# Register loads of table places, four at a time among a super's matmuls, and the residual input read behind the last super

## The chip, the cores and the metric

One core of a Trainium2 chip runs the whole kernel. The metric is the device time of one execution in microseconds (us). The kernel before was timed three times: 801.56, 800.24 and 801.06 us, median 801.06 us. The engines are TensorE (PE; PEld is its loading of weights), VectorE (DVE), ScalarE (ACT), GpSimd (POOL) and SyncE (SP, which here only issues DMAs). Each engine has a sequencer that reads its program, works on registers, waits for semaphores and hands work to the engine; a "q" behind an engine's name in a row (PEldq, SPq, DVEq) means a record of the sequencer.

## The reference

One layer of a graph network with a residual sum and a layer norm, on 6250 nodes of 256 features and 100,000 edges of 64 features:

```
sums   = segment_sum(edge_attr, src)                # 6250 x 64
counts = segment_sum(1, src)
agg    = sums / max(counts, 1)
h      = relu([x, agg, u[0]] @ W1 + b1)             # 448 -> 512
y      = h @ W2 + b2                                # 512 -> 256
out    = layernorm(x + y)
```

Everything is float32. The edge features are split into three bfloat16 parts that add up to the float32 value, so that matmuls with bfloat16 one-hot matrices sum them exactly.

## The kernel before

The nodes are held as 125 partitions by 50 columns; two columns together are a bucket (25 buckets). The kernel has four stages.

1. A short setup (to about 28 us) counts the edges of each bucket and works out where each group of up to four edges of a bucket goes.
2. The edge stage (to about 447 us) reads the edges in 44 chunks of 6 batches. For each batch PE sorts the rows with one-hot matmuls (line 858), ACT copies them out of PSUM and POOL scatters them with an indirect DMA to `sorted_rows` in DRAM, in order of bucket. Beside it PE multiplies the node features with the first 256 rows of W1 into `pre`.
3. The super stage (452.5 to 671.5 us) is the one that the change touches. A super is 128 sorted rows with four slots of one edge each, all of one bucket. There are 258 of them, in 129 pairs. SP reads a pair in one DMA of 396 KB (`super_turn` of SP, line 505, the issue at line 511). DVE writes one-hot matrices of 128 by 256 (line 1236; three for the first super of a pair and four for the second; ACT makes the one left, lines 713 and 716). PE adds the super's rows into the table in PSUM: per super 4 slots (`r`) x 2 halves of the nodes (`h`) x 3 parts = 24 matmuls (line 936), each with its own load of weights.
4. The last stage (to 799.5 us), 25 steps `g` of two columns: means, the edge part of the first layer, ReLU, second layer (line 990), residual sum and layer norm, and the stores.

**The order within the super stage.** PE, DVE and ACT each run 16 turns of a hardware loop, one turn being 16 supers (`BODY`), and two supers behind the loop. Where a super's sums go is a column of PSUM that is known only at run time. It is looked up in `where_row`, one partition of SBUF with 384 places for PE and as many row numbers for SP. At the head of each turn PE loads 16 places at once into 16 registers (`pe.load`, line 927). Then for each super: line 929 copies the place of this super from its register, line 930 waits for DVE's one-hots (`s_hot_d`), line 932 for ACT's in every first super of a pair, and the matmuls follow; the column of the second half (`h` = 1) is the place plus 512, computed between the third and the fourth matmul (recorded at line 936). The last matmul raises `s_added`. Four one-hot buffers (`HOT_BUFS`) stand between DVE and PE: DVE and ACT may write the one-hots of super n once super n - 4 is added (lines 1234 and 712). SP may read a pair into its buffer once the pair eight before it is added (line 510), and has its own loads of 8 row numbers per turn (`find_rows`, line 503).

**The residual input.** SP reads `x` again into `xs` (6.4 MB, in the layout of the output) during the super stage: from turn 3 on, behind the eight pairs of each turn, a piece of four columns in two DMAs (112 and 13 partitions, lines 524 to 528), and the last two columns at lines 530 to 532. All of them raise `s_xs`. POOL waits for all 13 pieces (line 614) and then adds `b2` to `xs`, column by column in place: `add_b2` (line 616, its additions at line 619) three steps ahead of the steps of the last stage. Between them POOL makes the low part of the hidden values for the second layer (`low_hidden`, line 628). DVE needs `xs` of a step at line 1296.

Of the kernel before, what the change touches and what calls it, by code (L numbers as in the profile page):

```python
# [9 lines left out]
I32 = mybir.dt.int32  # L10
# [7 lines left out]
P = 128  # L18
NODES, DIM = 6250, 256
# [5 lines left out]
NP = 125  # L25
COLS = NODES // NP
BUCKETS = COLS // 2
ROW = FEAT + 1
XPART = 112
# [35 lines left out]
SUPER_PAIRS = -(-SUPERS // 2)  # L65
# [8 lines left out]
SUPER_COLS = -(-SUPERS // P)  # L74
# [19 lines left out]
PAIR_BUFS = 8  # L94
HOT_BUFS = 4
BODY = 2 * PAIR_BUFS
SUP_TURNS = SUPER_PAIRS // PAIR_BUFS
ACT_SLOT = SLOTS - 1
TURN = 3
TURNS = CHUNKS // TURN  # L100
# [5 lines left out]
LOOKS = -(-(BATCHES - SOON) // LOOK)  # L106
assert LOOKS + 3 <= CHUNKS

X_TURN = 3
X_COLS = 4  # L110
X_PIECES = COLS // X_COLS
X_PIECE = X_COLS * DIM
B2_AHEAD = 3
Z_BUFS = 3
assert X_TURN + X_PIECES + 1 == SUP_TURNS

STEPS = COLS // 2
PAIR = 10
# [4 lines left out]
def build(nc, x, src, attr, u, w1, b1, w2, b2, out):  # L123
# [7 lines left out]
    x_v = x.rearrange("(p c) d -> p (c d)", p=NP)  # L131
# [4 lines left out]
    with ctx:  # L136
        def sb(name, shape, dt=F32):
            return ctx.enter_context(nc.sbuf_tensor(name, shape, dt))
# [7 lines left out]
        def sem(name):  # L146
            return ctx.enter_context(nc.semaphore(name))

        ident = sb("ident", [P, P])
        b2_all = sb("b2_all", [P, DIM])  # L150
        eps_col = sb("eps_col", [P, 1])
        where_row = sb("where_row", [1, 2 * SUPER_COLS * P], I32)
        node_of = sb("node_of", [P, 2 * P], I16)
        pre = sb("pre", [P, COLS * HID // P * NP])
        stats = sb("stats", [P, 2, 2, 6])
# [119 lines left out]
        xs = sb("xs", [P, COLS * DIM])  # L275
# [88 lines left out]
        s_apart = sem("s_apart")  # L364
        s_added = sem("s_added")
        s_table = sem("s_table")
        s_xs = sem("s_xs")
        s_xb = sem("s_xb")
        s_own_act = sem("s_own_act")
        s_own_dve = sem("s_own_dve")  # L370
# [33 lines left out]
        def _(sp):  # L404
# [100 lines left out]
            def super_turn(m, count=PAIR_BUFS, found=False):  # L505
                if not found:
                    find_rows(m, count)
                for k in range(count):
                    at = sp.snap(row_regs[k], min_val=0, max_val=ZERO_SUPER * P)
                    sp.wait_ge(s_added, m * BODY + (2 * k + 2))  # L510
                    sp.dma_start(sup_pair[k][:, :, :, :].rearrange("p s r w -> p s (r w)"),
                                 sorted_rows[bass.ds(at, 2 * P), :].rearrange("(s p) w -> p s w", p=P)
                                 ).then_inc(s_sup[k], 16)
# [4 lines left out]
                sp.wait_ge(s_sent[s], 16 * CHUNKS)  # L518

            super_turn(0, found=True)  # L520
            for m in range(1, X_TURN):
                super_turn(m)
            sp.wait_ge(s_pre, COLS + 1)
            with sp.Fori(X_TURN, X_TURN + X_PIECES) as m:
                super_turn(m)
                for lo, hi in ((0, XPART), (XPART, NP)):
                    sp.dma_start(xs[lo:hi, bass.ds(m * X_PIECE - X_TURN * X_PIECE, X_PIECE)],
                                 x_v[lo:hi, bass.ds(m * X_PIECE - X_TURN * X_PIECE, X_PIECE)]).then_inc(s_xs, 16)
            super_turn(X_TURN + X_PIECES)
            for lo, hi in ((0, XPART), (XPART, NP)):  # L530
                sp.dma_start(xs[lo:hi, X_PIECES * X_PIECE:COLS * DIM], x_v[lo:hi, X_PIECES * X_PIECE:COLS * DIM]
                             ).then_inc(s_xs, 16)
            super_turn(SUP_TURNS, SUPER_PAIRS - SUP_TURNS * PAIR_BUFS)

            def store_step(g, b):
                sp.wait_ge(s_out, g * 2 + 2)
# [10 lines left out]
        def _(pool):  # L547
# [63 lines left out]
                pool.wait_ge(s_w_hi, 3)  # L611
                nc.gpsimd.tensor_tensor(low, whole, high.bitcast(F32), ALU.subtract).then_inc(s_w_lo, 1)
            pool.wait_ge(s_b2, 16)
            pool.wait_ge(s_xs, 2 * 16 * (X_PIECES + 1))

            def add_b2(g):
                for c in range(2 * g, 2 * g + 2):
                    column_x = xs[0:NP, c * DIM:(c + 1) * DIM]
                    nc.gpsimd.tensor_tensor(column_x, column_x, b2_all[0:NP, :], ALU.add).then_inc(s_xb, 1)  # L619

            for g in range(B2_AHEAD):
                add_b2(g)
# [146 lines left out]
        def _(pe):  # L769
# [153 lines left out]

            table_regs = [pe.alloc_register(f"table_reg{k}") for k in range(BODY)]

            def super_turn(m, count=BODY):
                pe.load(table_regs[0:count], where_row[0:1, bass.ds(m * BODY, count)])
                for k in range(count):
                    at = pe.snap(table_regs[k], min_val=0, max_val=(PAIR_BANKS - 1) * 1024 + (BANK_COLS - 1) * ROW)
                    pe.wait_ge(s_hot_d, m * BODY + (k + 1))  # L930
                    if k % 2 == 0:
                        pe.wait_ge(s_hot_a, m * PAIR_BUFS + (k // 2 + 1))
                    for r in range(SLOTS):
                        for h in range(2):
                            for part, width in ((0, FEAT), (1, FEAT), (2, ROW)):
                                last = nc.tensor.matmul(ps[:, bass.ds(at + h * 512, width)],  # L936
                                                        onehot[k % HOT_BUFS][:, r, h * P:(h + 1) * P],
                                                        sup[k][:, r, part * PLANE:part * PLANE + width],
                                                        start=False, stop=False)
                    last.then_inc(s_added, 1)  # L940

            with pe.Fori(0, SUP_TURNS) as m:
                super_turn(m)
            super_turn(SUP_TURNS, 2 * SUPER_PAIRS - SUP_TURNS * BODY)
# [410 lines left out]
```

## Time and profile before

The page is of one profiled execution: its span (first to last instruction) is 799.5 us, 1.56 us (0.2%) under the median of the three runs; the profile lists no other time of that execution, so its span is the own time that it has. The mean granted clock of TensorE is 0.994 of 2.4 GHz.

| stretch | us | what bounds it by the busy shares |
|---|---|---|
| 60 to 250 (edges) | 190 | PE busy 187.85, DVE 188.60 |
| 250 to 460 (edges, end of them, start of supers) | 210 | PE busy 207.61 |
| 500 to 520 (supers) | 20 | PE busy 18.74, DVE 18.52, DMA share 0.92 |
| 680 to 800 (last stage) | 120 | PE 104.40, DVE 100.35, ACT 92.21, POOL 94.97 |

How to read it: a busy time is the union of an engine's instructions in the stretch. Matmuls are pipelined, so that one takes 193 ns and the next begins 31 ns behind it; where the text speaks of their rate it counts matmuls over a stretch. Instructions of a sequencer are not in the busy times. "Idle before" and what released an engine are inferred from semaphores; "issue" is a wait for nothing that the profile shows.

### The profile page before, as it was taken

The page shows a single profiled execution, that of the slowest core. Times are in us where ns is not written, and L with a number is a line of the kernel's source. Part 1 is how long each engine was busy: PE and PEld are TensorE (multiplying, and loading weights), DVE is VectorE, ACT ScalarE, POOL GpSimd, SP SyncE. Part 2 cuts the span into 40 slices and gives each one's busy share as a digit, 9 for nine tenths or more (in the row PEclk, how much of TensorE's full clock was granted, in tenths as well). Part 3 has the DMA queues.
Part 4 walks back from the last instruction along what each step waited for, and adds up shares of the span by engine and source line. Part 5 has one row for each costly group of instructions (what it writes and reads, how often), then busy time and mean ns, then how long its engine had stood idle before and what let it go on. Part 6 is the DMA issues. An engine that isn't in the chain of part 4 may idle for free.

```text
span 799.5 us, 31269 instructions
## 1 busy us (share of the span) xinstructions
PE 745.1 (93%) x11398; PEld 711.5 (89%) x11399; DVE 716.8 (90%) x2382; ACT 501.7 (63%) x998; POOL 417.1 (52%) x410
## 2 busy tenths in 40 slices
PE   8889999999999999999999888989898986899995
PEld 4689999999999999999999888989898986899995
DVE  8999999999999999999896388989898988799995
ACT  1366676666667767667667545555555552688886
POOL 3087777777677787877776400000000002788983
PEclk9999999999999999999999999999999999999999
DMA  6366556666665666656674678999999990012122
GB/s 215 131 210 204 201 202 211 213 215 219 202 219 195 212 220 211 225 205 214 203 210 167 239 227 260 281 282 282 285 283 285 281 277 10 27 52 64 53 66 64
DMA packets 75268, 156.38 MB, mean 196 GB/s; under 512 B 11084, under 2 KB 51277, under 8 KB 75097
## 3 DMA queue, kind: packets, MB, share of 16 engines
q1 hardware_dynamic: 58328, 102.33, 42.5%
q0 software_dynamic: 16896, 53.54, 17.9%
q8 instruction: 18, 0.29, 0.2%
q14 instruction: 26, 0.20, 0.1%
HBM read 95.47 MB, written 60.37 MB: 195 GB/s over the span
## 4 chain that ended last, share of the span: by engine, by line
PE 60%; DVE 30%; issue 5%; ACT 2%; POOL 1%; DMA 1%; DVEq 0%; ACTq 0%; SPq 0%; POOLq 0%
PE ps L858 33%; DVE onehot L1236 18%; PE ps L785 11%; PE ps L936 5%; PE ps L990 3%; DVE pre L1275 2%; DVE perm L1146 2%; DVE stats L1301 1%; DVE weights_z L1296 1%; PE ps L776 1%; PE ps L792 1%; POOL h_low L628 1%; PE ps L811 1%; PE ps L843 1%; PE ps L841 1%
## 5 line engine op out<-in xcount | busy, mean ns | idle before, releaser
L600 POOL DMA_INDIRECT sorted_rows<-payload,idx x264 | 304.8, 1155 | 131.8 <-issue 51.9
L858 PE MATMUL ps<-attr_buf,perm 128*128 128x198 bf16 x3168 | 302.6, 252 | 1.1 <-ACT attr_buf L642 0.8
L858 PEld LDWEIGHTS ps<-attr_buf,perm 128*128 128x128 bf16 x3168 | 288.6, 96 | 6.1 <-ACT attr_buf L642 1.2
L649 ACT CAST payload<-ps 128x792 bf16<-128x792 f32 x264 | 217.9, 825 | 76.7 <-PE ps L858 62.2
L1146 DVE TENSOR_SCALAR perm<-place_of,pos 128x512 bf16<-128x512 int16 x792 | 241.1, 362 | 3.4 <-PE ps L858 2.7
L1236 DVE TENSOR_SCALAR onehot<-node_of,sup 128x256 bf16<-128x256 int16 x903 | 192.4, 284 | 41.9 <-PE ps L936 22.3
L936 PE MATMUL ps<-sup,onehot 128*128 128x64 bf16 (+1 forms) x6192 | 196.1, 193 | 24.7 <-DVE onehot L1236 21.0
L936 PEld LDWEIGHTS ps<-sup,onehot 128*128 128x128 bf16 x6192 | 193.5, 98 | 27.3 <-issue 27.3
L619 POOL TENSOR_TENSOR xs<-xs,b_all 125x256 f32<-125x256 f32 x50 | 37.6, 775 | 209.4 <-DMA xs<-in_x 209.4
L713 ACT ACTIVATE apart<-node_of,sup 128x256 bf16<-128x256 int16 x129 | 65.6, 508 | 94.3 <-PE ps L936 90.2
L785 PE MATMUL ps<-xt,w1x 128*128 128x125 f32 x800 | 99.9, 278 | 5.9 <-DVE pos L1067 3.3
L785 PEld LDWEIGHTS ps<-xt,w1x 128*128 128x128 f32 x800 | 93.2, 192 | 10.8 <-issue 4.6
L660 ACT ACTIVATE pre<-ps,hid_bias 128x125 f32 (+1 forms) x200 | 56.7, 368 | 61.7 <-PE ps L785 61.7
L628 POOL TENSOR_TENSOR h_low<-pre,h_high 128x500 fp32r<-128x500 f32 x50 | 62.8, 1278 | 32.7 <-ACT pre L737 32.7
L1056 DVE TENSOR_TENSOR attr_buf<-attr_buf 128x576 f32<-128x576 f32 x88 | 65.8, 749 | 7.8 <-DMA attr_buf<-in_edge_attr 7.8
L1062 DVE TENSOR_TENSOR attr_buf<-attr_buf 128x576 f32<-128x576 f32 x88 | 65.4, 744 | 0.0
L716 ACT ACTIVATE onehot<-apart 128x256 bf16<-128x256 bf16 x129 | 53.8, 417 | 4.1
L990 PE MATMUL ps<-w_high,h_high 128*125 128x256 f32 x200 | 49.8, 282 | 1.0 <-issue 0.5
L990 PE MATMUL ps<-w_low,h_high 128*125 128x256 f32 x200 | 49.5, 280 | 0.0
L990 PE MATMUL ps<-w_high,h_low 128*125 128x256 f32 x200 | 34.1, 292 | 7.6 <-POOL h_low L628 7.6
L990 PEld LDWEIGHTS ps<-w_high,h_high 128*125 128x125 f32 x200 | 37.1, 185 | 1.3 <-issue 0.7
L990 PEld LDWEIGHTS ps<-w_low,h_high 128*125 128x125 f32 x200 | 37.2, 186 | 0.0
(150 smaller groups left out, 603.7 us busy)
## 6 DMA issues: line engine op xcount, KB each, us to landing
sup<-sorted_rows SPq DMA_DIRECT2D x129, 396.0 KB, 4.0
attr_buf<-in_edge_attr SPq DMA_DIRECT2D x43, 576.0 KB
out<-weights_z SPq DMA_DIRECT2D x25, 224.0 KB
xs<-in_x SPq DMA_DIRECT2D x12, 448.0 KB
x_stage<-in_x SPq DMA_DIRECT2D x47, 112.0 KB
sorted_rows<-payload,idx POOLq DMA_INDIRECT x264
pre<-jump_d SPq DMA_DIRECT2D x1, 1560.0 KB, 10.4
pre<-first_d SPq DMA_DIRECT2D x1, 780.0 KB, 7.2
```

The costliest lines, as they stand in the source:

```text
L600: pool.indirect_dma_start(out=sorted_rows, out_offset=bass.IndirectOffsetOnAxis(ap=idx[:, n:n + 1], axis=0), in_=payload[s][:, :], in_offs ...
L628: nc.gpsimd.tensor_tensor(h_r[b][1][:, at:end], pre[:, g * KH * NW + at:g * KH * NW + end], h_r[b][0][:, at:end].bitcast(F32), ALU.subtrac ...
L649: nc.scalar.copy(payload[s][:, :].rearrange("p (r w) -> p r w", w=PART), slots_p[s % PSUM_BUFS]).then_inc(s_pay, 1)
L713: nc.scalar.activation(apart[k // 2 % 2][:, :], node_of[:, :], ACT.Abs, scale=-1.0, bias=place_in[k][:, ACT_SLOT, :]).then_inc(s_apart, 1)
L785: last = nc.tensor.matmul(pre_p[b][:, k * NP:(k + 1) * NP], w1x[:, c, k * P:(k + 1) * P], xt[b][:, c, :], start=(c == 0), stop=(c == KX - 1))
L858: last = nc.tensor.matmul(slot_p[s % PSUM_BUFS][r].rearrange("p (h f) -> p h f", f=PLANE), places, parts(a, t * CB + s), start=(t == 0 and ...
L936: last = nc.tensor.matmul(ps[:, bass.ds(at + h * 512, width)], onehot[k % HOT_BUFS][:, r, h * P:(h + 1) * P], sup[k][:, r, part * PLANE:pa ...
L990: last = nc.tensor.matmul(y_p[b][0:NP, c * DIM:(c + 1) * DIM], h_r[b][part][:, at:at + NP], w2r[w_part][:, k * DIM:(k + 1) * DIM], start=( ...
L1056: nc.vector.tensor_tensor(left, whole, high, ALU.subtract).then_inc(s_rest, 1)
L1062: nc.vector.tensor_tensor(low, left, middle, ALU.subtract).then_inc(s_low, 1)
L1146: last = nc.vector.tensor_scalar(perm[s][:, t, :], place_of[:, :], pos[:, bass.ds(c * CT + (t * CB + s), 1)], None, ALU.is_equal)
L1236: last = nc.vector.tensor_scalar(onehot[k % HOT_BUFS][:, r, :], node_of[:, :], place_in[k][:, r, :], None, ALU.is_equal)
```

## The change

It has two parts. **The places:** the load of 16 registers at the head of a turn is gone. `find_tables` loads four registers. It runs once ahead of the loop (supers 0 to 3), and in each turn behind the first slot (`r` = 0, six matmuls) of supers 2, 6, 10 and 14, each time for the four supers that begin two supers later; the one in super 14 loads for the next turn, and that of the last turn serves the two supers behind the loop. So there are 65 loads of four in place of 16 of sixteen and one of two. `where_row` is placed first in SBUF, and three small tiles behind it. **The residual input:** SP's reads of `x` in the turns are gone, and its turns 1 to 15 are one loop. Behind the last pair it reads `x` in five pieces of ten columns, two DMAs each, with a semaphore for each piece; POOL waits for a piece when `add_b2` comes to its first step.

```diff
--- before.py
+++ after.py
@@ -95,6 +95,8 @@
 HOT_BUFS = 4
 BODY = 2 * PAIR_BUFS
 SUP_TURNS = SUPER_PAIRS // PAIR_BUFS
+PLACES_AT_ONCE = 4
+assert 2 * SUPER_PAIRS - SUP_TURNS * BODY <= PLACES_AT_ONCE
 ACT_SLOT = SLOTS - 1
 TURN = 3
 TURNS = CHUNKS // TURN
@@ -106,13 +108,12 @@
 LOOKS = -(-(BATCHES - SOON) // LOOK)
 assert LOOKS + 3 <= CHUNKS
 
-X_TURN = 3
-X_COLS = 4
+X_COLS = 10
 X_PIECES = COLS // X_COLS
 X_PIECE = X_COLS * DIM
 B2_AHEAD = 3
 Z_BUFS = 3
-assert X_TURN + X_PIECES + 1 == SUP_TURNS
+assert X_PIECES * X_COLS == COLS and X_COLS % 2 == 0 and X_COLS // 2 >= B2_AHEAD
 
 STEPS = COLS // 2
 PAIR = 10
@@ -146,10 +147,10 @@
         def sem(name):
             return ctx.enter_context(nc.semaphore(name))
 
+        where_row = sb("where_row", [1, 2 * SUPER_COLS * P], I32)
         ident = sb("ident", [P, P])
         b2_all = sb("b2_all", [P, DIM])
         eps_col = sb("eps_col", [P, 1])
-        where_row = sb("where_row", [1, 2 * SUPER_COLS * P], I32)
         node_of = sb("node_of", [P, 2 * P], I16)
         pre = sb("pre", [P, COLS * HID // P * NP])
         stats = sb("stats", [P, 2, 2, 6])
@@ -364,7 +365,7 @@
         s_apart = sem("s_apart")
         s_added = sem("s_added")
         s_table = sem("s_table")
-        s_xs = sem("s_xs")
+        s_xs = [sem(f"s_xs{k}") for k in range(X_PIECES)]
         s_xb = sem("s_xb")
         s_own_act = sem("s_own_act")
         s_own_dve = sem("s_own_dve")
@@ -518,19 +519,15 @@
                 sp.wait_ge(s_sent[s], 16 * CHUNKS)
 
             super_turn(0, found=True)
-            for m in range(1, X_TURN):
+            with sp.Fori(1, SUP_TURNS) as m:
                 super_turn(m)
+            super_turn(SUP_TURNS, SUPER_PAIRS - SUP_TURNS * PAIR_BUFS)
+
             sp.wait_ge(s_pre, COLS + 1)
-            with sp.Fori(X_TURN, X_TURN + X_PIECES) as m:
-                super_turn(m)
+            for k in range(X_PIECES):
                 for lo, hi in ((0, XPART), (XPART, NP)):
-                    sp.dma_start(xs[lo:hi, bass.ds(m * X_PIECE - X_TURN * X_PIECE, X_PIECE)],
-                                 x_v[lo:hi, bass.ds(m * X_PIECE - X_TURN * X_PIECE, X_PIECE)]).then_inc(s_xs, 16)
-            super_turn(X_TURN + X_PIECES)
-            for lo, hi in ((0, XPART), (XPART, NP)):
-                sp.dma_start(xs[lo:hi, X_PIECES * X_PIECE:COLS * DIM], x_v[lo:hi, X_PIECES * X_PIECE:COLS * DIM]
-                             ).then_inc(s_xs, 16)
-            super_turn(SUP_TURNS, SUPER_PAIRS - SUP_TURNS * PAIR_BUFS)
+                    sp.dma_start(xs[lo:hi, k * X_PIECE:(k + 1) * X_PIECE], x_v[lo:hi, k * X_PIECE:(k + 1) * X_PIECE]
+                                 ).then_inc(s_xs[k], 16)
 
             def store_step(g, b):
                 sp.wait_ge(s_out, g * 2 + 2)
@@ -611,9 +608,10 @@
                 pool.wait_ge(s_w_hi, 3)
                 nc.gpsimd.tensor_tensor(low, whole, high.bitcast(F32), ALU.subtract).then_inc(s_w_lo, 1)
             pool.wait_ge(s_b2, 16)
-            pool.wait_ge(s_xs, 2 * 16 * (X_PIECES + 1))
 
             def add_b2(g):
+                if g % (X_COLS // 2) == 0:
+                    pool.wait_ge(s_xs[g // (X_COLS // 2)], 2 * 16)
                 for c in range(2 * g, 2 * g + 2):
                     column_x = xs[0:NP, c * DIM:(c + 1) * DIM]
                     nc.gpsimd.tensor_tensor(column_x, column_x, b2_all[0:NP, :], ALU.add).then_inc(s_xb, 1)
@@ -923,8 +921,10 @@
 
             table_regs = [pe.alloc_register(f"table_reg{k}") for k in range(BODY)]
 
+            def find_tables(k, at):
+                pe.load(table_regs[k:k + PLACES_AT_ONCE], where_row[0:1, bass.ds(at, PLACES_AT_ONCE)])
+
             def super_turn(m, count=BODY):
-                pe.load(table_regs[0:count], where_row[0:1, bass.ds(m * BODY, count)])
                 for k in range(count):
                     at = pe.snap(table_regs[k], min_val=0, max_val=(PAIR_BANKS - 1) * 1024 + (BANK_COLS - 1) * ROW)
                     pe.wait_ge(s_hot_d, m * BODY + (k + 1))
@@ -937,8 +937,12 @@
                                                         onehot[k % HOT_BUFS][:, r, h * P:(h + 1) * P],
                                                         sup[k][:, r, part * PLANE:part * PLANE + width],
                                                         start=False, stop=False)
+                        if r == 0 and k % PLACES_AT_ONCE == 2 and count == BODY:
+                            following = k - 2 + PLACES_AT_ONCE
+                            find_tables(following % BODY, m * BODY + following)
                     last.then_inc(s_added, 1)
 
+            find_tables(0, 0)
             with pe.Fori(0, SUP_TURNS) as m:
                 super_turn(m)
             super_turn(SUP_TURNS, 2 * SUPER_PAIRS - SUP_TURNS * BODY)
```

## Rows read from the trace of the kernel before

**Rows 1.** The page: engines' busy time; DMA in 40 slices of 20 us

```profile
PE 745.1 (93%) x11398; PEld 711.5 (89%) x11399; DVE 716.8 (90%) x2382; ACT 501.7 (63%) x998; POOL 417.1 (52%) x410
DMA  6366556666665666656674678999999990012122
GB/s 215 131 210 204 201 202 211 213 215 219 202 219 195 212 220 211 225 205 214 203 210 167 239 227 260 281 282 282 285 283 285 281 277 10 27 52 64 53 66 64
```

**Rows 2.** Waits from 450 to 670 us: total us, times, longest

```profile
PEld ps L936 <- issue: 27.3, 21, 1.8
DVE onehot L1236 <- PE ps L936: 22.3, 17, 1.4
```

**Rows 3.** Line 936 in two turns: width; PE, PEld busy; clock; DMA share; GB/s

```profile
483.05:496.33 13.28, 12.03 (x384) 11.88 (x385) 1.00 0.81 243
496.33:509.57 13.24, 11.98 (x384) 11.86 (x385) 1.00 0.89 280
```

**Rows 4.** One seam, one body: PE, PEld, DVE, ACT, POOL busy; clock; DMA

```profile
494.89:496.33 1.44, 0.19 (x6) 0.07 (x4) 1.08 (x6) 0.42 (x1) 0.00 (x0) 1.00 0.99 326
496.33:508.15 11.82, 11.82 (x384) 11.82 (x384) 10.71 (x52) 6.99 (x15) 0.00 (x0) 1.00 0.90 281
```

**Rows 5.** Timeline (start, us); the first two from the window 494.38 to 496.58

```profile
494.20 0.87 PE L936 MATMUL ps<-sup,onehot 128*128 128x64 bf16 x23
496.33 0.42 PE L936 MATMUL ps<-sup,onehot 128*128 128x64 bf16 x7 [1.25 <-DVE onehot L1236]
497.32 11.91 DVE L1236 TENSOR_SCALAR onehot<-node_of,sup 128x256 bf16<-128x256 int16 x56 [1.33 <-PE ps L936]
```

**Rows 6.** Lines 942, 927, 929, 936 in narrow windows: ns; start, once each

```profile
L942 PEldq ALU_OP  x1: 32/32/32, 494.4 to 494.4; - x1
L942 PEldq FUSED_REGOPS  x1: 65/65/65, 494.7 to 494.7; - x1
L927 PEldq TENSOR_LOAD <-where_row x1: 1105/1105/1105, 494.9 to 494.9; - x1
L929 PEldq FUSED_REGOPS  x1: 41/41/41, 496.0 to 496.0; - x1
L929 PEldq FUSED_REGOPS  x1: 41/41/41, 496.6 to 496.6; - x1
L936 PEldq FUSED_REGOPS  x1: 51/51/51, 497.6 to 497.6; - x1
```

**Rows 7.** Register loads (ns min/median/max) of 16, 2, 8, 8 and 1 registers

```profile
L927 PEldq TENSOR_LOAD <-where_row x13: 1102/1107/1127, 468.3 to 627.5; - x13
L927 PEldq TENSOR_LOAD <-where_row x1: 556/556/556, 669.0 to 669.0; - x1
L503 SPq TENSOR_LOAD <-where_row x3: 533/537/538, 453.8 to 482.5; - x3
L503 SPq TENSOR_LOAD <-where_row x12: 691/696/706, 497.2 to 642.9; - x12
L503 SPq TENSOR_LOAD <-where_row x1: 507/507/507, 655.8 to 655.8; - x1
```

**Rows 8.** Timeline of the last supers

```profile
655.55 6.87 PE L936 MATMUL ps<-sup,onehot 128*128 128x64 bf16 x216 [1.29 <-DVE onehot L1236]
656.54 12.97 DVE L1236 TENSOR_SCALAR onehot<-node_of,sup 128x256 bf16<-128x256 int16 x49 [1.37 <-PE ps L936]
657.41 0.41 SPq L511 DMA_DIRECT2D sup<-sorted_rows  x1
660.18 4.15 POOL L619 TENSOR_TENSOR xs<-xs,b_all 125x256 f32<-125x256 f32 x6 [209.40 <-DMA xs<-in_x]
669.96 1.69 PE L936 MATMUL ps<-sup,onehot 128*128 128x64 bf16 x48 [0.47 <-DVE onehot L1236]
```

**Rows 9.** Timeline of the last stage's first step

```profile
683.00 2.75 POOL L628 TENSOR_TENSOR h_low<-pre,h_high 128x500 fp32r<-128x500 f32 x2 [18.67 <-ACT pre L737]
686.64 0.76 DVE L1296 TENSOR_TENSOR weights_z<-ps,xs 125x256 f32<-125x256 f32 x2 [2.02 <-PE ps L990]
```

## The prediction

> **What bounds the kernel now.** I read the page's busy times first: PE is at 93%, DVE at 90% [rows 1], so a stage has to be looked at by itself. The change touches the super stage, and I went to its waits: 21 idle spells of PE's weight loads, 27.3 us in sum, of which the profile can name no releaser, and 17 of DVE on PE, 22.3 us [rows 2]. Sixteen turns stand against these counts, so I took the turns: one is 13.24 to 13.28 us for 384 matmuls [rows 3]. Cut at the seam, it is 11.82 us of unbroken matmuls, 11.82 / 384 = 30.8 ns each, and 1.44 us from the last start to the next, one pitch of 0.03 included: 1.41 us of stall [rows 4]. The row calls DVE's one-hots the releaser, but DVE has four buffers written by then and is itself waiting for PE (its block begins 0.99 us behind PE's) [rows 5]; the wait is the register load, 1105 ns, which stands exactly in the gap [rows 6]. DVE needs 11.91 us for its 56 instructions of a turn [rows 5], PE 11.82: away from the seam they are level, and PE has no slack in which a new stall could vanish.
>
> How far is PE's sequencer ahead of its matmuls? I looked each record up in windows of 0.01 to 0.02 us, which gives the hundredths that its row rounds off [rows 6]. Its first record of the seam (line 942) is at 494.38, and the last matmul of the turn starts at 494.20 + 0.87 - 0.19 = 494.88: 0.50 us, 16 matmuls. Behind the seam it reaches line 929 of the second super at 496.58, when 7 matmuls of the first super's 24 have started: 17 are left [rows 5, 6]. The two agree, and a lead of 17, or 17 x 0.0308 = 0.52 us, is all that can cover a stop of the sequencer.
>
> **The seam.** Without the load, line 929 runs where the load began, at 494.87 in place of 496.03 [rows 6]: 1.16 us less, and 1.41 - 1.16 = 0.25 us of stall stay, since the branch and the register operations take more than the lead by themselves. Fifteen seams give 15 x 1.16 = -17.4 us. The sixteenth had a load of two registers, 556 ns [rows 7], before a block with 0.47 us of idle time [rows 8]: -0.6. The first load of all lies beside PE's wait for the first one-hots; I count nothing for it.
>
> **The loads among the matmuls.** There are 4 per turn, 64 in all. In each the sequencer leaves line 929 with 17 matmuls ahead, spends 0.33 us (497.32, which is 496.58 and one super of 24 x 0.0308 us, to 497.65 [rows 6]) to get to the place + 512 of this super, and passes on its last three matmuls of the first slot. Then PE has work until 0.52 + 6 x 0.031 = 0.71 us behind line 929, that is 0.38 us behind the record at 497.65. In that time it needs 0.12 us for this record and the matmuls behind it, 0.12 us for the load's address (the step from line 942's register operation at 494.75 to the load at 494.87), the load L, and 0.05 us to the next matmul (the load ends at 495.97, the next record is 0.06 later) [rows 6]. The stall is 0.29 + L - 0.38 = L - 0.09 us. The change asks for the load at the worst place of a super: just behind the register work, when the lead has been eaten.
>
> The trace has no load of four. Through PE's two sizes, 556 ns for 2 and 1107 for 16, the line gives 0.635; through SP's 507 for 1 and 696 for 8 it gives 0.588 [rows 7]. I take 0.61, the middle: 0.52 us of stall, 64 x 0.52 = +33.3 us. The bounds: one register takes 507 ns, eight in a loop 696 [rows 7], and the address may be ready without an operation of its own (-0.12). So the stall is 0.30 to 0.61 us, +19 to +39 us. The new place of `where_row` changes only its address; whether that shortens a load is inside the bounds.
>
> Behind PE's load stand, on PE, the remaining 18 matmuls of the super and with them `s_added`, for which DVE, ACT and SP wait. None of them gets a bound of its own: DVE is asked for 11.91 us in a turn that becomes 11.82 + 4 x 0.52 + 0.25 = 14.15 us.
>
> **The residual input.** In the turns SP loses 13 pieces of two DMAs, and gains nothing: a turn without them is 13.28 us at 243 GB/s, one with them 13.24 at 280 [rows 3], so they cost nothing where they were and their removal gives nothing. PE's slower turns ask the DMA queues for less still. Behind the last pair SP issues ten DMAs. The last pair's issue is at 657.41, over 12 us before PE's last block [rows 8]; with the shift of 14 us that is 671. The eight pairs that may be on their way are 3.2 MB and the input 6.4 MB, at the 283 GB/s of the slices [rows 1] 11 and 22.6 us: first piece by 671 + 11 + 4.5 = 687, last by 705. POOL's six first additions took 4.15 us [rows 8], so they end at 691, before `low_hidden` of step 0 at 683 + 14 = 697 and DVE's residual sum at 686.64 + 14 = 701 [rows 9]. The second piece is wanted for step 5 and lands by 692. POOL waited until 660.18 before [rows 8], too, so its order is the same. This costs nothing.
>
> One small gain lies here. While POOL added those six columns, DVE's one-hots took 12.97 / 49 = 265 ns in place of 11.91 / 56 = 213 [rows 5, 8], and the sixteen supers from 655.55 to the last block's start at 669.96 took 14.41 us, where 11.82 and the last stall are 12.3 [rows 4, 8]: 2.1 us lost. After the change the additions run again near the end, but PE then leaves DVE more than 2 us of slack per turn. I take -1.0, with 0 and -2 as its bounds.
>
> **The sum.** +33.3 - 17.4 - 0.6 - 1.0 = +14.3 us. The profiled execution has a span of 799.5 us and would come to 813.8; the runs' median, 801.06, lies 1.56 us over that span, and 801.06 + 14.3 = 815.4. I say 815. The bounds together: 19.2 - 17.4 - 0.6 - 2 = -0.8, and 39.0 - 17.4 - 0.6 = +21: 800 to 822, a turn being break-even at a stall of 17.4 / 64 = 0.27 us plus the two small terms, 0.30.
>
> **The rivals.**
>
> The loads are hidden (the faster side). It decides at one point: while a load runs, do the 18 matmuls behind it still get to PE, or is the lead longer than I read? For it: none of the 18 uses a register that the load fills, whereas in the trace every load is followed at once by an operation that needs its result, so that no row shows a load being passed. Against it: those matmuls take their column from a register, each record of the sequencer on rows 6 begins only when the one before has ended, and the lead of 17 was found twice. Its price: no 33.3, so -17.4 - 0.6 - 1.0 = -19, 782 us; should the 0.25 at the seams go as well, DVE's 11.91 us would be the turn, 15 x (13.24 - 11.91) = -20, 779.
>
> Two statements of the Trainium skill stand on that side. "Advanced Engine Details and Errata", section Sequencer Loop, says that other engine instructions can be read and queued while microcode runs a control instruction. No row here shows it. "TensorE: Matmul & The Clock Gate", in its table of the engine, gives TensorE's queue as 64 deep, which is 32 pairs of weight load and matmul, about 0.99 us of lead; by it the stall of this seam would have been some 0.5 us shorter than the 1.41 us of rows 4, so the trace goes against it, and by it the stall of a load of four would be near 0.05 us.
>
> The loads cost what the seams gave (no change). A load of 0.51 us with its address ready makes the stall 0.30 and the sum about 0: 800 to 802 us. For it: SP took 507 for one register and 537 ns for eight in the unrolled turns [rows 7]. Against it: the loops' loads are slower, and the new ones are in a loop.
>
> The input comes too late. If the first piece is not there by 697, every us beyond goes to the end. It would need a delay of 6 us (687 and 4.15 of additions against 697) with POOL in order; for it speaks that the reads now wait for the end of the super stage, against it all that is worked out above. A delay of 10 us would give 815 + 4 = 819.
>
> **How the numbers follow.** The forecast 0.71; hidden loads 0.18; no change 0.08; late input 0.03. 0.2%, 1.6 us, is what a measurement of this kernel can tell. Slower by more than that: 0.71 + 0.03 + 0.02 of the third case = 0.76; within it 0.06; faster 0.18. The range takes in the bounds of the load and the third case and leaves the hidden loads out: 799 to 823. It holds 8 in 10.
>
> **What would show it.** In the trace after: 65 register loads on PE of 0.5 to 0.7 us (0.61 expected); PE's blocks of matmuls cut at supers 2, 6, 10 and 14 of a turn, behind the sixth matmul, by 0.3 to 0.6 us each; the seam's stall down to about 0.25 us; a turn of about 14.15 us; DVE's longest spells of work cut where PE's are; the DMA share in the supers down from 0.89 [rows 3] to about 0.75; POOL's first additions around 680 to 690 and no wait of DVE for them. I am wrong if PE's matmuls run on through the loads: then the turn is near 12 us and the time near 782. I am wrong in size if a load of four is far from 0.61 us, 0.1 us of it being 6.4 us of the whole.

## The result and the profile after

The changed kernel takes 793.95 us (median of 4 runs, 793.33 to 794.84) against 801.31 us of the kernel before beside it (800.24 to 801.59): ratio 0.9909, 95% interval 0.9894 to 0.9924, 7.4 us faster. The forecast was 815 us, within 799 to 823. The profiled execution took 793.33 us, its span is 791.2 us; before it was 799.5.

The page's rows after, which answer to [rows 1]: TensorE is busier, and the DMA share in the supers (slices 24 to 33) is lower.

```profile
PE 754.5 (95%) x11398; PEld 713.8 (90%) x11399; DVE 717.3 (91%) x2382; ACT 501.8 (63%) x998; POOL 409.2 (52%) x410
...
DMA  6366666666666666666565488888888889512122
GB/s 217 114 213 212 204 201 213 213 199 213 219 201 229 217 206 206 205 218 228 200 200 189 166 276 255 249 255 251 254 249 253 255 248 240 132 53 66 54 66 65
```

The waits of the super stage (total us, times, longest), which answer to [rows 2]: TensorE's loads of weights now wait 12.1 us in 50 spells in place of 27.3 in 21, and DVE waits for PE 2.6 us in place of 22.3.

```profile
PEld ps L936 <- issue: 12.1, 50, 1.8
DVE onehot L1240 <- PE ps L936: 2.6, 4, 1.7
```

Line 936 in two turns, columns as in [rows 3]: a turn is 12.9 us, not 14.15.

```profile
483.40:496.30 12.90, 12.60 (x390) 12.12 (x387) 1.00 0.84 247
496.33:509.15 12.82, 12.56 (x389) 12.07 (x386) 1.00 0.84 257
```

The register loads of PE's sequencer (ns, least, median, most) with the operation that makes their address, which answer to [rows 6, 7]. This is where the forecast broke: 332 ns, not 610.

```profile
L925 PEldq FUSED_REGOPS  x60: 46/46/51, 463.2 to 653.8; - x60
L925 PEldq TENSOR_LOAD <-where_row x60: 328/332/352, 463.3 to 653.9; - x60
```

PE's loads of weights around such register loads. The idle time in brackets runs from the end of one load of weights, which takes 0.10 us and overlaps the next by 0.07, so 0.07 us have to be added for the time that PE lost: 0.22 to 0.26 us each. Blocks of 96 matmuls are four supers, cut where the change loads. This view joins two blocks when the idle time between them is short; the third row holds a stop of this size that it doesn't show, so one block is not yet a proof that nothing stopped.

```profile
560.90 3.00 PEld L936 LDWEIGHTS ps<-sup,onehot 128*128 128x128 bf16 x96 [0.19 <-issue]
564.08 3.02 PEld L936 LDWEIGHTS ps<-sup,onehot 128*128 128x128 bf16 x96 [0.18 <-issue]
567.25 6.36 PEld L936 LDWEIGHTS ps<-sup,onehot 128*128 128x128 bf16 x192 [0.15 <-issue]
573.77 1.32 PEld L936 LDWEIGHTS ps<-sup,onehot 128*128 128x128 bf16 x41 [0.16 <-issue]
```

The branch at the end of the loop (line 942 before, 946 now), first and last start of 16. Their distance is 15 turns: (661.5 - 468.2) / 15 = 12.89 us after, (668.9 - 467.9) / 15 = 13.40 before. Taken one by one, the turns before are 13.2 to 13.3 us, but the last, with POOL's additions in it [rows 8], 15.2; after, all fifteen are 12.8 to 13.0. I use this row as the measure of a turn for every kernel below.

```profile
L946 PEldq COMPARE_BRANCH  x16: 76/208/219, 468.2 to 661.5; - x16
```

```profile
L942 PEldq COMPARE_BRANCH  x16: 76/208/219, 467.9 to 668.9; - x16
```

The seam, read in windows of 0.1 us (width; PE, PEld busy with their counts; clock; DMA share; GB/s), here the one whose branch starts at 494.0. PE's loads of weights stand still for 0.11 us (0.09 in the middle window, 0.02 in the last), with the 0.07 a stall of 0.18 us. Eleven seams read so have 0.16 to 0.22 us, 0.19 in the mean.

```profile
494.40:494.50 0.10, 0.10 (x8) 0.10 (x4) 1.00 1.07 301
494.50:494.60 0.10, 0.10 (x5) 0.01 (x1) 1.00 0.65 238
494.60:494.70 0.10, 0.10 (x5) 0.08 (x3) 1.00 1.08 206
```

The super stage, from the first to the last of its matmuls, went from 219.0 us (452.5 to 671.5) to 210.8. Of the 8.2 us, 7.7 are in the fifteen turns (201.0 to 193.3) and 0.7 behind them (2.6 to 1.9 us); the first turn, from the first matmul to the branch, is 0.2 longer.

```profile
L936 PE MATMUL ps<-sup,onehot x6192: 189/193/204, 452.6 to 663.4; 128*128 128x64 bf16 x134, 128*128 128x65 bf16 x66
```

Its end answers to [rows 8, 9]. The ten DMAs of the residual input are issued at 651.45, and POOL's first six additions run from 662.93 to 667.06, behind the last one-hots (661.30); `low_hidden` follows at 675.15.

```profile
648.87 12.43 DVE L1240 TENSOR_SCALAR onehot<-node_of,sup 128x256 bf16<-128x256 int16 x54
...
651.45 5.45 SPq L529 DMA_DIRECT2D xs<-in_x  x10
...
662.93 4.13 POOL L617 TENSOR_TENSOR xs<-xs,b_all 125x256 f32<-125x256 f32 x6 [211.71 <-DMA xs<-in_x]
...
675.15 1.33 POOL L626 TENSOR_TENSOR h_low<-pre,h_high 128x500 fp32r<-128x500 f32 x1 [8.10 <-ACT pre L735]
```

### The profile page after: what moved, and what is told of

The parts are those of the page before. It is cut to its first block, busy times and chain, and to the rows that moved or that the text cites. A ratio compares the mean times of both kernels' runs of the same rounds, so it can differ in the third digit from the quotient of the medians.

```text
span 791.2 us, 31310 instructions
## 1 busy us (share of the span) xinstructions
PE 754.5 (95%) x11398; PEld 713.8 (90%) x11399; DVE 717.3 (91%) x2382; ACT 501.8 (63%) x998; POOL 409.2 (52%) x410
## 4 chain that ended last, share of the span: by engine, by line
PE 58%; DVE 32%; issue 5%; ACT 2%; POOL 1%; DMA 1%; DVEq 0%; ACTq 0%; SPq 0%; POOLq 0%
PE ps L936 26%; PE ps L856 17%; DVE perm L1150 13%; PE ps L783 6%; DVE attr_buf L1066 4%; DVE attr_buf L1060 4%; PE ps L994 4%; DVE pre L1279 2%; DVE pos L1071 2%; DVE stats L1305 1%; DVE weights_z L1300 1%; DVE picked L1137 1%; POOL h_low L626 1%; DVE chosen L1134 1%; PE ps L790 1%
## 5 line engine op out<-in xcount | busy, mean ns | idle before, releaser
L597 POOL DMA_INDIRECT sorted_rows<-payload,idx x264 | 296.4, 1123 | 140.1 <-ACT payload L647 56.9
L1240 DVE TENSOR_SCALAR onehot<-node_of,sup 128x256 bf16<-128x256 int16 x903 | 195.5, 282 | 30.2 <-DMA sup<-sorted_rows 16.6
L936 PE MATMUL ps<-sup,onehot 128*128 128x64 bf16 (+1 forms) x6192 | 204.0, 193 | 8.3 <-issue 2.4
L936 PEld LDWEIGHTS ps<-sup,onehot 128*128 128x128 bf16 x6192 | 195.9, 97 | 16.5 <-issue 12.1
```

Source lines behind the costliest of these rows:

```text
L597: pool.indirect_dma_start(out=sorted_rows, out_offset=bass.IndirectOffsetOnAxis(ap=idx[:, n:n + 1], axis=0), in_=payload[s][:, :], in_offs ...
L1240: last = nc.vector.tensor_scalar(onehot[k % HOT_BUFS][:, r, :], node_of[:, :], place_in[k][:, r, :], None, ALU.is_equal)
```

## The experiments

The first four kernels ran on one chip, the next four on another, the last four on a third. On these the kernel before took 844 to 848 us (medians): in all their traces the supers begin 40 to 50 us later, and the reason stays open. The super stage, which all this is about, is as before: `e4_before_where_first`, with the old loads and the old input, has 218.7 us and a mean turn of 13.40, and `e3_where_old`, with both parts of the change, 211.1 us and 12.90. So I read turns and widths across chips, and times only against the kernel before on the same chip.

### The two parts alone

```diff
# e1_places_only: the kernel before with the places' part of the change (excerpt)
-                pe.load(table_regs[0:count], where_row[0:1, bass.ds(m * BODY, count)])
+        where_row = sb(...)                 # first tile
+                        if r == 0 and k % PLACES_AT_ONCE == 2 and count == BODY:
+                            ...         # find_tables, as in the change
# e2_input_only: the changed kernel, where_row in its old place, no find_tables (excerpt)
+                pe.load(table_regs[0:count], where_row[0:1, bass.ds(m * BODY, count)])
```

> The loads of four and where_row first in SBUF; the residual input is read in the turns as before. Theory (the places are all of the gain but some 2 us, which the earlier input reads cost through POOL's additions beside the one-hots): turns of 12.86 us as in the changed kernel, the last supers again slowed; 795 to 796 us against 794 of the change. Rival (the input part brings half of the gain): 797 to 798 us.

> The input in five pieces behind the last super; the places loaded sixteen at the head of a turn, where_row in its old place. Theory: turns stay at 13.25 us, only the lost 2 us at the last supers come back: 799 to 800 us. Rival (half of the gain): 797 us.

Measured: the places alone 0.9932 (0.9908 to 0.9956) of the kernel before, 841.85 against 847.84 us; the input alone 1.0000 (0.9972 to 1.0028), 846.12 us. For the places that is as expected (795 to 796 of 801 us); the time of the input part cannot be told from nothing. The traces are sharper. The stage's widths are 212.8 us and 215.9 us (this row of each), against 218.7 in `e4_before_where_first` below, on the same chip, which has the old loads and the old input.

```profile
L939 PE MATMUL ps<-sup,onehot x6192: 189/193/245, 496.4 to 709.2; 128*128 128x64 bf16 x134, 128*128 128x65 bf16 x66
```

```profile
L934 PE MATMUL ps<-sup,onehot x6192: 190/193/203, 502.6 to 718.5; 128*128 128x64 bf16 x134, 128*128 128x65 bf16 x66
```

These widths hold the first turn too, which took 14.2 us in the input alone, 15.1 in `e4_before_where_first` and 16.0 in the places alone, before any input is read, so they are off by up to 1 us each way. The fifteen turns between the branches are free of that: 194.9 us for the places alone, 199.1 for the input alone, 201.0 for neither and 193.5 for both (`e3_where_old`). So the places alone are worth 6.1 us of them, the input alone 1.9, and both together 7.5. The input's 1.9 us are in the last turn: with the old input it takes 15.1 us and the others 13.2 to 13.4, with the new one all take 13.2 to 13.3. I had put this effect at 1 us. In the timeline of the last supers of the places alone, POOL adds for 4.15 us while DVE is still at the one-hots, and PE has a gap of 0.92 us whose releaser is DVE; with the input alone POOL begins at 716.92, behind the last one-hots, and PE's last full turn is one block.

```profile
691.89 15.80 DVE L1243 TENSOR_SCALAR onehot<-node_of,sup 128x256 bf16<-128x256 int16 x59
...
699.54 4.15 POOL L620 TENSOR_TENSOR xs<-xs,b_all 125x256 f32<-125x256 f32 x6 [204.73 <-DMA xs<-in_x]
...
703.23 0.94 PE L939 MATMUL ps<-sup,onehot 128*128 128x64 bf16 x24 [0.92 <-DVE onehot L1243]
```

```profile
704.43 12.08 PE L934 MATMUL ps<-sup,onehot 128*128 128x64 bf16 x384 [1.25 <-DVE onehot L1234]
...
705.44 10.50 DVE L1234 TENSOR_SCALAR onehot<-node_of,sup 128x256 bf16<-128x256 int16 x49 [1.35 <-PE ps L934]
...
716.92 4.14 POOL L617 TENSOR_TENSOR xs<-xs,b_all 125x256 f32<-125x256 f32 x6 [216.87 <-DMA xs<-in_x]
```

### Is it the address or the number of registers?

```diff
# e3_where_old: the changed kernel, where_row behind eps_col again
# e4_before_where_first: the kernel before, where_row as the first tile
```

> The changed kernel with where_row back in its old place in SBUF, nothing else. Theory (how long a load takes hangs on the address of what it reads): PE's loads of four rise from 332 ns to 500 or more, each stall from 0.24 to 0.41 us or more, 64 x 0.17 = +11 us, some 805 us. Rival (it hangs on the number of registers alone): 332 ns and 794 us.

> The kernel before with where_row first in SBUF, nothing else. Theory (address): the load of sixteen falls well below 1107 ns, by 0.3 to 0.6 us, and every seam by as much: 15 x that is 5 to 9 us, 792 to 797 us. Rival (number of registers alone): 1107 ns and 801 us.

Measured: the changed kernel with the tile in its old place 840.40 us, 0.9918 (0.9884 to 0.9953) of the kernel before; the kernel before with the tile first 846.61 us, 0.9977 (0.9945 to 1.0009). Each load is as long as at the other place. My theory that the tile's place explains 332 ns fell, and the rival (the number of registers) held as far as it was tried here.

```profile
L925 PEldq TENSOR_LOAD <-where_row x65: 328/332/512, 495.1 to 704.8; - x65
```

```profile
L927 PEldq TENSOR_LOAD <-where_row x17: 556/1106/1300, 498.3 to 716.3; - x17
```

SP's loads do differ between the kernels, but with the input part: 696 ns for eight registers before [rows 7], 524 after, and 283 for the one register at the end, where it was 507.

```profile
L504 SPq TENSOR_LOAD <-where_row x14: 521/524/528, 469.8 to 637.2; - x14
```

```profile
L504 SPq TENSOR_LOAD <-where_row x1: 283/283/283, 649.9 to 649.9; - x1
```

The loads of turns 1 to 3 of the kernel before, which follow no input read, had 537 already [rows 7]; the third of them lies in the loop, so it isn't the loop that makes a load longer, as I had taken it. A load on SP directly behind the DMAs of the input is some 170 to 220 ns longer; the places alone and `e4_before_where_first`, which keep these DMAs, have about 695 too, and the kernels without them 523 to 526 where the address is a multiple of four elements; the cause was not tried in another way.

### What a load costs by its size, and where it lies

```diff
# at8_r1 (excerpt)
+PLACES_AT_ONCE = 8
+                        if r == 1 and k % PLACES_AT_ONCE == 6 and count == BODY:
# at2_r0 (excerpt)
+PLACES_AT_ONCE = 2
+                        if r == 0 and k % PLACES_AT_ONCE == 0 and count == BODY:
# shift1 (excerpt; the values are written from element 1 on, SP's loads shifted as well)
+        where_row = sb("where_row", [1, 2 * SUPER_COLS * P + 4], I32)
+                pe.load(table_regs[k:k + PLACES_AT_ONCE], where_row[0:1, bass.ds(at + 1, PLACES_AT_ONCE)])
```

> The changed kernel with two loads of eight per turn behind r = 1 of supers 6 and 14. It prices a load by its size. Theory (332 ns for four and 258 for each further four, which gives 1106 for sixteen): 0.59 us for eight, two stalls of about 0.26 us. Rival (fixed time plus little per register, as SP's 507 for one and 524 for eight): about 0.35 us for eight and no stall.

> The changed kernel with eight loads of two per turn, behind r = 0 of every first super of a pair. Theory (time goes in steps of four registers): 332 ns for two as for four, eight stalls of 0.23 us, a turn of 13.8 us. Rival (64.5 ns per register, the line through 4 and 16): 203 ns for two, stalls of 0.11 us, a turn of 12.9 us.

> The changed kernel with the 768 values in where_row one element (4 bytes) further on, and all loads on PE and SP reading them there. Theory (a load goes by aligned groups of four registers, 258 ns each and 74 ns for the whole; two registers took 535, so what isn't such a group goes one by one): a load of four is about 1.05 us (or 0.59 us where it is two groups), the stall 0.5 to 0.96 us, a turn of 13.9 to 15.7 us. Rival (four registers cost 332 ns wherever they lie): 332 ns and 12.86 us.

Measured: eight registers 592 ns, two 537, and four that begin one element further on 1002. The whole times, one run each, are 837.82, 877.50 and 882.62 us.

```profile
L925 PEldq TENSOR_LOAD <-where_row x33: 587/592/767, 496.7 to 703.3; - x33
```

```profile
L925 PEldq TENSOR_LOAD <-where_row x129: 533/537/721, 491.0 to 743.2; - x129
```

```profile
L925 PEldq TENSOR_LOAD <-where_row x65: 997/1002/1188, 498.4 to 748.3; - x65
```

Sixteen took 1107, four 332. The ones that begin at a multiple of four elements and fill whole fours lie on one line: 332, 592, 1107 are 74 + 258 for each four. Two (537) and the shifted four (1002) lie on another, 72 + 233 for each register. So the times read as a load that goes in fours where the address is a multiple of four elements, and one by one elsewhere, at nearly the price of a whole four. The theory of fours fitted eight registers (592 ns for an expected 590). Both theories for two registers missed (332 and 203 ns expected), and from that came the theory for the shifted four, which foretold 1.05 us. The address does matter after all, but only within a group of four; by this reading the tile begins at a multiple of four elements in either of its places, since both gave 332 ns. One shift, by one element, is all that was tried. SP's loads, shifted as well, went from 525 to 1672 ns for eight; the turn of that kernel (below) is what PE's stalls give, so they held nothing up.

The stalls went with the loads. Behind r = 0 they are 0.42 to 0.46 us for the load of two and 0.89 to 0.93 for the shifted four, where L - 0.09 (L is the load's time) says 0.45 and 0.91; the mean turns are 15.65 and 15.59 us. With two registers one load of a turn stands in the first super behind the seam, where the lead (how far the sequencer is ahead of PE) is used up; its stall is 0.56 + 0.07 = 0.63 us, the third row. Behind r = 1 the two loads of eight stall PE by 0.32 to 0.37 us, not by the 0.26 expected, and the turn is 12.67 us.

```profile
566.05 1.55 PEld L936 LDWEIGHTS ps<-sup,onehot 128*128 128x128 bf16 x48 [0.35 <-issue]
567.95 1.55 PEld L936 LDWEIGHTS ps<-sup,onehot 128*128 128x128 bf16 x48 [0.35 <-issue]
...
574.07 1.53 PEld L936 LDWEIGHTS ps<-sup,onehot 128*128 128x128 bf16 x48 [0.56 <-issue]
```

```profile
577.85 3.25 PEld L936 LDWEIGHTS ps<-sup,onehot 128*128 128x128 bf16 x96 [0.82 <-issue]
581.96 3.00 PEld L936 LDWEIGHTS ps<-sup,onehot 128*128 128x128 bf16 x96 [0.86 <-issue]
```

### Does the sequencer stand still?

```diff
# twice: the call repeated
+                            find_tables(following % BODY, m * BODY + following)
# twice2 (excerpt): a second load, into registers that every other super uses
+                pe.load(other_regs[other:other + PLACES_AT_ONCE], where_row[0:1, bass.ds(at, PLACES_AT_ONCE)])
+  at = pe.snap(table_regs[k] if k % 2 == 0 else other_regs[k % (2 * PLACES_AT_ONCE)], ...)
```

> The changed kernel with each load of four done twice in a row, behind r = 0. It tells whether the sequencer stands still in a load. Theory (it does, and the lead is used up by the first): each of the four stalls of a turn grows by the whole second load and its address, 0.33 + 0.12 us, from 0.23 to 0.68 us, and a turn from 12.86 to 14.66 us. Rival (matmuls pass a load, and the 0.23 us come from something else): a turn grows by less than 0.5 us.

The trace of `twice` has 65 loads, not 129: the repeated load, whose first result nobody reads, is not in the program that ran. Its turn, 12.90 us, is that of the changed kernel, and it says nothing on the question.

> The changed kernel, each load of four at r = 0 followed by a second load of the same four places into other registers, which every other super uses (the earlier double load was left with 65 loads in its program, so it doubled nothing). Theory (the sequencer stands still in a load and the lead is used up by the first): each of the four stalls of a turn grows from 0.23 us by 0.33 and 0.06 to 0.12 us to about 0.65 us, a turn from 12.86 to about 14.5 us. Rival (matmuls pass a load): a turn grows by less than 0.5 us.

Measured: 65 loads at each of the two lines, 857.51 us (one run). A turn is (726.1 - 509.2) / 15 = 14.46 us, the stalls 0.55 + 0.07 = 0.62 us.

```profile
L950 PEldq COMPARE_BRANCH  x16: 83/215/234, 509.2 to 726.1; - x16
```

```profile
562.59 3.02 PEld L940 LDWEIGHTS ps<-sup,onehot 128*128 128x128 bf16 x96 [0.54 <-issue]
566.18 3.21 PEld L940 LDWEIGHTS ps<-sup,onehot 128*128 128x128 bf16 x96 [0.56 <-issue]
```

The second load, 0.33 us and its register operation, is in the stall whole: 0.62 us against 0.22 to 0.26. No matmul that stands behind a load reaches PE before the load ends, though the 18 of this super don't use what it reads. They do take their column from another register; matmuls with a fixed column were not tried.

### Where among the matmuls

```diff
# r1, r2: r == 1, r == 2 in place of r == 0
# r2h0: in the loop over h
+                            if r == 2 and h == 0 and k % PLACES_AT_ONCE == 2 and count == BODY:
```

> The changed kernel with each load of four one slot later (behind r = 1, the twelfth matmul of the super). Theory (stall = the sequencer's 0.29 us + L - what it is ahead; PE has no other cost): the lead at that place is some 17 matmuls, 0.52 us, against 0.12 + 0.33 + 0.05 = 0.50 us, so the four stalls of a turn go from 0.23 us each to nearly nothing and a turn from 12.86 to about 12.0 us, 15 to 16 turns x 0.86 = -13 us against the changed kernel, about 21 us (2.6%) under the kernel before. Rival (VectorE or another engine takes over at once): turns stay above 12.5 us, at most -5 us.

> The changed kernel with each load of four behind the eighteenth matmul (all of r = 2). Theory (two hurdles): the load itself finds the full lead and does not stall, but only 6 matmuls are left for the next super's register work, so the stall of about 0.1 us comes one super later; a turn of about 12.2 to 12.3 us. Rival (only the place before the load counts): no stall, 12.1 us or less.

> The changed kernel with each load of four behind the fifteenth matmul of the super (first half of r = 2). In the run behind r = 1 the stalls of about 0.10 and 0.07 us were left, at the load, since the lead was only 0.39 us there. Theory (two hurdles, the load's 0.50 us and the next super's 0.33 us of register work, share one lead of 0.52 us that fills again in between): at this place about 0.48 us of lead meet the load and 9 matmuls, 0.28 us, are left for the next super's register work; stalls of 0.05 us or less, a turn of 12.1 us against 12.31 behind r = 1 and 12.86 of the change. Rival (VectorE's 11.91 us and what it waits at the seam are the floor already): turns stay at 12.3 us.

Measured: behind the twelfth matmul 826.91 us, 0.980 (0.972 to 0.988) of the kernel before on the same chip; behind the eighteenth 824.78 (one run, 843.59 before); behind the fifteenth 827.49 us, 0.983 (0.976 to 0.990). The times of these three cannot be told apart; the turns can: 12.31, 12.15 and 12.02 us. Behind the twelfth the expectation (12.0) missed: (12.31 - 11.82 - 0.19 of the seam) / 4 leaves 0.08 us per load, since the sequencer has not got its full lead back by then. One load of `r1` bears this out: it begins at 546.60, the last matmul before the gap starts at 546.82, so that some 0.25 us of matmuls were left, where the full lead of 0.52 us less the 0.12 for the address would be 0.40. Behind the eighteenth a turn is 0.13 us longer than behind the fifteenth, 0.03 us per load, less than the 0.1 us that I had expected and not the nothing of the rival. Behind the fifteenth the turn is a little under the 12.1 us expected: the load and the next super's register work each find enough of the lead.

```profile
L946 PEldq COMPARE_BRANCH  x16: 76/208/227, 510.7 to 695.3; - x16
```

```profile
L946 PEldq COMPARE_BRANCH  x16: 76/208/227, 510.8 to 693.0; - x16
```

```profile
L946 PEldq COMPARE_BRANCH  x16: 76/208/227, 512.3 to 692.6; - x16
```

All three are under the changed kernel's 12.89, and 12.02 is 11.82 of matmuls and a seam of 0.2. The 30 us around two of its seams are one block for the profile, at 30.17 / 965 = 31.3 ns per matmul. The block alone would not show it, since `r1` has such blocks too; in windows of 0.05 us from 530 to 580 the only stops of PE's loads of weights in `r2h0` are at the seams (0.16 to 0.21 us of stall), while `r1` has stops at its register loads as well (0.08 to 0.11 us).

```profile
574.92 30.17 PEld L936 LDWEIGHTS ps<-sup,onehot 128*128 128x128 bf16 x965
```

The super stage of `r2h0` is 198.1 us (496.4 to 694.5), 12.7 under the changed kernel's 210.8, and its fifteen turns 180.3 against 193.3. By the turns it is the best version found. In time it is 0.983 of the kernel before, where the change is 0.991, each on its own chip; the two were not timed side by side, and their intervals touch. `r1` has a neighbour on its own chip: `twice`, whose program has the loads of the changed kernel and its turn, took 837.99 us (one run), and the four runs of `r1` 824.30 to 832.35.

## Why the prediction was wrong

**What bounds the kernel** was right: a stop of PE's sequencer beyond the lead is time lost, and turns from 12.02 to 15.65 us were made by the size, number and place of the loads alone.

**The stall's formula**, 0.29 + L - 0.38 us behind r = 0, was right: for L of 0.33, 0.54 and 1.00 us it says 0.24, 0.45 and 0.91, and the stalls were 0.22 to 0.26 (most of them 0.22), 0.42 to 0.46 and 0.89 to 0.93. The lead of 17 matmuls also led to the best place.

**The step that failed** is the size of L: "Through PE's two sizes, 556 ns for 2 and 1107 for 16, the line gives 0.635; through SP's 507 for 1 and 696 for 8 it gives 0.588. I take 0.61, the middle". A load of four is 332 ns, a stall 0.24 us instead of 0.52, and 64 of them some 15 us instead of 33.3. The two points of PE's line belonged to two different lines: two registers one by one, sixteen as four groups of four. The bound under it failed as well: "one register takes 507 ns" was a load behind the input's DMAs, and took 283 without them. The 696 ns for eight "in a loop" were of the same kind: the loop's first load, in turn 3, had 538. Nothing in the trace said that a load of fewer registers must be shorter than one of more in the same way; I drew a line through two points and took its end for a floor. With 0.332 the same sum is 15.5 - 17.4 - 0.6 - 1.0 = -3.5 us, below the range.

**The seam** was expected to shrink by 1.16 us each, to a stall of 0.25. It is 0.19 us in the mean of the windows above, and the turns agree: of 12.89 us, 11.82 are matmuls and 4 x 0.22 the loads' stalls, which leaves 0.19. The copy of a place (line 929) went from 256 records of register operations and 2 moves to the counts below: sixteen fewer, and at the seam, where it had one between branch and wait [rows 6], the trace after has none. That this copy is the difference was not tried by itself. Fifteen times 0.06 us is -0.9.

```profile
L929 PEldq FUSED_REGOPS  x176: 41/41/46, 452.8 to 659.7; - x176
L929 PEldq MOVE  x66: 29/37/38, 455.5 to 662.2; - x66
```

**The residual input** cost nothing, as said. Its first piece was there 11.5 us behind its issue (651.45 to 662.93; predicted were 16), but that is late enough that POOL's additions left the one-hots alone altogether, 1.9 us gained instead of 1 (2 was the bound that I had named), and they ended 8 us before `low_hidden` (predicted: 6).

**What is left.** In the fifteen turns the sum with 0.332 is 60 stalls of 0.24, 15 seams of -1.16 and the -1.0 of the additions, -3.9 us; measured are -7.7. The seams give -0.9 more, the loads -1.2 (60 times 0.22 in place of 0.24), the last turn -0.9, which makes -6.9; 0.8 us stay without a name. Behind the turns the -0.6 for the load of two was -0.7. In the first turn, where four stalls had been counted, the two kernels differ by 0.2 us, and since runs with the same loads differ there by 1 us, nothing can be read from it.

**The chance.** The faster side had 0.18, all on matmuls passing a load. It came by another way, a cheap load, to which I had given no chance of its own; the prediction only named the stall of 0.30 us at which the change breaks even.

"Advanced Engine Details and Errata" of the Trainium skill, section Sequencer Loop, says that other engine instructions can be read and queued while a control instruction is worked on. `twice2` shows that these matmuls are not. "TensorE: Matmul & The Clock Gate" of the Trainium skill, in its table of the engine, gives TensorE's queue as 64 deep, by estimate 32 pairs or 0.99 us of lead. With that, the loads of 0.33 us would have left no stall behind r = 0; the runs show 0.22 us and more. "DMA: Bandwidth & Descriptors" of the Trainium skill, in its section on latency and other measured facts, gives a floor of about 600 ns for a `tensor_load`. The runs go down to 332 ns on PE and 283 on SP.

## What to carry to other kernels

Price a sequencer operation at the size and address at which it will run, or give it a range that reaches to nothing: two sizes make no line, and an aligned group of four registers costs less (332 ns) than two (537). Count how many matmuls the sequencer is ahead at the very place where the operation is put: the same load cost 0.22 to 0.26 us behind the 6th matmul of a super, 0.08 behind the 12th and nothing that the windows show behind the 15th. A stop is best put where the queue has just filled and enough matmuls are left for the next stretch of register work.

## What the runs showed of the hardware

- A register load from SBUF by PE's sequencer: 74 ns and 258 for each four that begins at a multiple of four elements (332, 592 and 1107 ns for 4, 8 and 16); 72 and 233 for each single one (537 for 2, 1002 for 4 begun one element further on).
- PE's sequencer was 16 to 17 pairs of weight load and matmul ahead before [rows 5, 6], and the stalls behind the sixth matmul in the changed kernel, `at2_r0`, `shift1` and `twice2` fit this lead (0.22 to 0.93 us).
- Matmuls whose column comes from a register did not pass a register load: a second load of 0.33 us made each stall some 0.38 us longer (`twice2`).
- The seam of PE's hardware loop, with its branch of 208 ns, stalled PE by 0.16 to 0.22 us with no load in it.
- Additions of 125 x 256 float32 by POOL beside DVE's one-hots took 4.15 us; the one-hots of the block around them took 265 ns on average in place of 213, and the last turn was 1.9 us longer.
- A register load on SP directly behind the input's DMAs took 170 to 220 ns more than one that is not (696 against 524 ns for eight registers, 507 against 283 for one).
